# Moving the softmax division of the last stage from the weights to the weighed heads, with transposed reciprocals

## What is computed

```python
def attention(q, k, v, mask):
    scores = jnp.einsum('bhqd,bhkd->bhqk', q, k) / jnp.sqrt(jnp.float32(HD))
    scores = scores * mask - 10000.0 * (1.0 - mask)
    probs = jax.nn.softmax(scores, axis=-1)
    return jnp.einsum('bhqk,bhkd->bhqd', probs, v)
...
ctx = merge_heads(attention(split_heads(q), split_heads(k), split_heads(v), ltor_mask))
attn_out = ctx @ w_ao + b_ao
x = hidden_states + attn_out
...
ctx = merge_heads(attention(split_heads(q), split_heads(k), split_heads(v), cross_mask))
cross_out = ctx @ w_co + b_co
x = x + cross_out
```

## Time and profile before

| | |
|---|---|
| median of 3 runs | 1036.88 us (1036.30 to 1036.94) |
| profiled execution, its own time | 1035.47 us |
| its span in the trace | 1034.2 us |
| PE, PEld busy | 1000.6 us (97%), 900.8 us (87%) |
| DVE, ACT, POOL busy | 767.9 us (74%), 577.0 us (56%), 651.7 us (63%) |
| granted TensorE clock, mean | 1.00 |

### The profile page before, as it was taken

The page is one execution under the profiler, slowest core; times in us unless marked ns, Lnnn a source line. Parts: engine busy times, 40 slices in busy tenths (PEclk is TensorE's granted clock), DMA queues, the critical chain, the costliest instruction groups (busy, mean ns, idle before and its releaser), DMA issues.

```text
span 1034.2 us, 21141 instructions
## 1 busy us (share of the span) xinstructions
PE 1000.6 (97%) x8239; PEld 900.8 (87%) x8239; DVE 767.9 (74%) x1229; ACT 577.0 (56%) x1288; POOL 651.7 (63%) x595
## 2 busy tenths in 40 slices
PE   7899999999999999999998999999998999989998
PEld 7788888888899999999997999999998988777877
DVE  7997888998257677876767867777865387898761
ACT  5998888797534422223233332222226489999982
POOL 6885476755578574434367666755534388999960
PEclk9999999999999999999999999999999999999999
DMA  8200001000121220121120111110120000000000
GB/s 329 119 2 2 1 2 42 2 1 2 47 77 42 72 82 28 56 82 42 41 85 21 42 42 42 34 38 12 31 103 1 1 2 1 2 2 2 12 11 21
DMA packets 33931, 40.73 MB, mean 39 GB/s; under 512 B 2127, under 2 KB 31273, under 8 KB 32297
## 3 DMA queue, kind: packets, MB, share of 16 engines
q1 hardware_dynamic: 33833, 39.38, 11.4%
HBM read 38.32 MB, written 1.05 MB: 38 GB/s over the span
## 4 chain that ended last, share of the span: by engine, by line
PE 81%; POOL 9%; DVE 4%; ACT 4%; issue 1%; DMA 0%; SPq 0%; DVEq 0%; ACTq 0%; POOLq 0%
PE psum L914 11%; PE psum L793 9%; PE psum L809 9%; PE psum L946 8%; PE psum L994 8%; PE psum L981 6%; PE psum L928 5%; PE psum L960 5%; PE psum L835 5%; POOL C tile L1792 3%; PE psum L720 3%; PE psum L970 3%; PE psum L825 3%; PE psum L850 2%; POOL C tile L1798 2%; PE psum L864 1%
## 5 line engine op out<-in xcount | busy, mean ns | idle before, releaser
L1929 POOL TENSOR_TENSOR B tile<-B tile,B rec 128x1024 f32<-128x1024 f32 x32 | 61.0, 1909 | 161.6 <-DVE B rec L1351 161.6
L1798 POOL TENSOR_TENSOR A tile<-A tile,outer rec 128x1024 f32<-128x1024 f32 x48 | 91.0, 1905 | 57.9 <-DVE outer rec L1190 57.8
L1655 ACT COPY B PT<-psum 128x512 f32<-128x512 f32 x64 | 32.9, 601 | 139.0 <-PE psum L970 139.0
L1072 DVE TENSOR_SCALAR B qT<-psum,cols 128x1024 f32<-128x1024 f32 (+1 forms) x38 | 44.0, 1166 | 71.6 <-PE psum L914 70.2
L1570 ACT ACTIVATE A tile<-A tile,outer min 128x128 f32<-128x128 f32 (+1 forms) x256 | 92.2, 448 | 2.6 <-DVE outer min L1183 2.5
L1570 ACT ACTIVATE C tile<-C tile,outer min 128x128 f32<-128x128 f32 x256 | 77.9, 399 | 0.5 <-DVE outer min L1183 0.4
L946 PE MATMUL psum<-B v hi,cT hi 128*128 128x256 f32 x256 | 72.1, 282 | 0.3 <-ACT B kT L1485 0.3
L946 PE MATMUL psum<-B v hi,cT lo 128*128 128x256 f32 x256 | 71.8, 281 | 0.0
L946 PE MATMUL psum<-B v lo,cT hi 128*128 128x256 f32 x256 | 71.8, 281 | 0.0
L1798 POOL TENSOR_TENSOR C tile<-C tile,outer rec 128x1024 f32<-128x1024 f32 x32 | 60.5, 1895 | 6.0 <-DVE outer rec L1190 6.0
L1176 DVE TENSOR_TENSOR A tile<-m,psum 128x1024 f32<-128x1024 f32 x48 | 56.5, 1216 | 9.2 <-PE psum L825 8.0
(11 more groups left out here) (327 smaller groups left out, 3470.5 us busy)
## 6 DMA issues: line engine op xcount, KB each, us to landing
weights<-in_weights_c SPq DMA_DIRECT2D x5, 1024.0 KB, 6.3
raw<-in_wq SPq DMA_DIRECT2D x32, 128.0 KB, 2.7
raw<-in_wk SPq DMA_DIRECT2D x32, 128.0 KB, 3.0
raw<-in_wv SPq DMA_DIRECT2D x16, 256.0 KB, 2.8
raw<-in_wo SPq DMA_DIRECT2D x16, 256.0 KB, 2.7
weights<-in_weights_a SPq DMA_DIRECT2D x1, 3072.0 KB, 21.6
weights<-in_weights_a SPq DMA_DIRECT2D x1, 2048.0 KB, 12.4
wide<-in_bias_v SPq DMA_DIRECT2D x2, 1024.0 KB, 10.3
```

The costliest lines, as they stand in the source:

```text
L1798: pool.tensor_tensor(tile(u, ly.nk), tile(u, ly.nk), part.rec[:, u % 4, 0:ly.per].unsqueeze(2).to_broadcast([P, ly.per, ly.nk]), ALU.mult) ...
L1929: pool.tensor_tensor(tv, tv, m.brec[:, h, :].unsqueeze(2).to_broadcast([P, B, S]), ALU.mult).then_inc(s["normalised"].sem, s["normalised"] ...
```

## The change

In stage C the exponentials are transposed undivided: `turn` waits for ACT's exponentials alone. POOL no longer multiplies the tile; it spreads the 8 reciprocals of a half over rec_rows (queries by head features), in two copies of 128 x 64. PE transposes the two 128 x 128 blocks of rec_rows in `weigh`, behind the products, into the other half of bank 6, after a wait for POOL's copies of both halves. ACT copies that half of the bank to rec_rows (128 x 256) in place of the two copies with bias, and DVE multiplies the heads in PSUM by it into OT (128 x 256). The values' bias, which no longer goes into OT, is multiplied by the output weights once (`rows`: four matmuls on PE, one addition on DVE of 128 x 512) and added to the output's rows. `rows 4` is put ahead of `turn_in M2 mlp 0` on PE, and `output 3` is moved ahead of it too. DVE's list gets 16 `weigh` steps. Stage A is as before.

```diff
@@
-HEADS_ON = {"A": "DVE", "C": "ACT"}
+HEADS_ON = {"A": "DVE", "C": "DVE"}
@@
+            self.Cs.rec_rows = sc("C rec rows", [P, 2, C, P])
@@
     "PE": """
-    output 0, output 1, output 2, turn_in M2 mlp 0 7, output 3, turn_in M2 mlp 1 1, up M2 0 0 4, up M2 0 2 5, up M2 0 4 1, up M2 0 6 2,
+    output 0, output 1, output 2, output 3, rows 4, turn_in M2 mlp 0 7, turn_in M2 mlp 1 1, up M2 0 0 4, up M2 0 2 5, up M2 0 4 1, up M2 0 6 2,
@@
     "DVE": """
...
+    stats M2 mlp 2, stats M2 mlp 3, rows 4, xn M2 mlp 2, turn_in M2 mlp 2 1, down M2 0 0 2, down M2 0 1 1, stats L3s in 0, xn M2 mlp 3, xn L3s in 0,
...
+    scores 2, turn_in L3s in 2 7, minima 2, weigh 0, scores 3, weigh 1, project 0 4, even 2 0, q L3s 2 0, minima 3, even 2 1, scores 4, even 3 0,
...
+    minima 12, weigh 11, project 10 2, project 11 1, turn_in L3c mlp 1 0, stats L3c in 3, even 12 0, xn L3c in 3, down L3c 0 0 3, minima 13,
+    down L3c 0 1 7, even 12 1, even 13 0, q L3c 3 2, even 13 1, scores 14, minima 14, weigh 12, scores 15, project 12 4, even 14 0, minima 15,
+    even 14 1, weigh 13, project 13 7, even 15 0, stats L3c mlp 2, even 15 1, xn L3c mlp 2, turn_in L3c mlp 2 2, weigh 14, down L3c 1 0 0,
+    project 14 7, down L3c 1 1 1, weigh 15, project 15 7, stats L3c mlp 3, xn L3c mlp 3, turn_in L3c mlp 3 7, down L3c 2 0 1, down L3c 3 0 2,
@@ PE
         def turn(n, r):
-            pe.wait_ge(s["evened"].sem, s["evened"].at((st, u)))
+            ready = "exp_made" if st == "C" else "evened"
+            pe.wait_ge(s[ready].sem, s[ready].at((st, u)))
@@ weigh
+            if st == "C":
+                pe.wait_ge(s["evened"].sem, s["evened"].at((st, 2 * n + 1)))
+                for c in range(C):
+                    i = pe.transpose(bank(6)[:, (C + c) * P:(C + c + 1) * P], part.rec_rows[:, n % 2, c, :], m.ident[:, :])
@@
+        def rows(z):
+            once("w_late_loaded", 32)
+            claim(z, "rows_made", "rows")
+            for n, name in enumerate(("L3s", "L3c")):
+                for c in range(C):
+                    i = pe.matmul(bank(z)[:, n * D:(n + 1) * D], layers[name].bv[:, c:c + 1].to_broadcast([P, P]), layers[name].wo[:, c, :],
+                                  start=c == 0, stop=c == C - 1)
@@ DVE
+            if st == "C" and n >= 2:
+                dve.wait_ge(s["evened"].sem, s["evened"].at((st, u - 4)))
@@ heads
+            if st == "C":
+                dve.wait_ge(s["rec_copied"].sem, s["rec_copied"].at(("C", n)))
+                dve.tensor_tensor(part.OT[b][:, :, :], bank(6)[:, 0:C * P].rearrange("p (c q) -> p c q", c=C), part.rec_rows[:, n % 2, :, :], ALU.mult).then_inc(
+                    s["heads_drained"].sem, s["heads_drained"].mark((ly.name, k, b)))
+                return
@@ ACT
+            elif what == "weigh" and st == "C":
+                act.wait_ge(s["weighed"].sem, s["weighed"].at((st, a[0])))
+                act.copy(part.rec_rows[:, a[0] % 2, :, :], bank(6)[:, C * P:2 * C * P].rearrange("p (c q) -> p c q", c=C)).then_inc(
+                    s["rec_copied"].sem, s["rec_copied"].mark((st, a[0])))
@@ POOL, even
+            if st == "C":
+                if n >= 2:
+                    pool.wait_ge(s["heads_drained"].sem, s["heads_drained"].at((units[n - 2][0].name, *units[n - 2][1:3])))
+                for c in range(C):
+                    i = pool.tensor_copy(part.rec_rows[:, n % 2, c, r * 4 * HD:(r + 1) * 4 * HD].rearrange("p (j q d) -> p j q d", j=2, q=2),
+                                         part.rec[:, u % 4, :].rearrange("p (j c q) -> p j c q", j=2, c=C)[:, :, c, :].unsqueeze(3).to_broadcast([P, 2, 2, HD]))
+                i.then_inc(s["evened"].sem, s["evened"].mark((st, u)))
+                return
```

More of the change, by code:

```diff
@@ L176 @@
     "bq_drained", "bk_drained", "bv_drained", "bshifted", "own_made", "summed", "normalised", "ot_hi", "ot_lo", "o_projected",
-    "o_added", "x_biased",
+    "o_added", "x_biased", "rows_projected", "rows_made", "rec_copied",
     "product_made", "product_copied", "products_added", "form_made", "forms_hi", "forms_lo", "half_made", "half_ended", "halves_hi", "halves_lo",
@@ L612 @@
     output 0, stats M2 mlp 0, output 1, xn M2 mlp 0, stats M2 mlp 1, output 2, xn M2 mlp 1, turn_in M2 mlp 0 7, output 3, turn_in M2 mlp 1 1,
-    stats M2 mlp 2, stats M2 mlp 3, xn M2 mlp 2, turn_in M2 mlp 2 1, down M2 0 0 2, down M2 0 1 1, stats L3s in 0, xn M2 mlp 3, xn L3s in 0,
-    turn_in L3s in 0 2, q L3s 0 1, scores 0, scores 1, minima 0, down M2 1 0 5, minima 1, down M2 1 1 1, stats L3s in 1, turn_in M2 mlp 3 7, xn L3s in 1,
-    even 0 0, even 0 1, turn_in L3s in 1 5, down M2 2 0 4, even 1 0, down M2 2 1 7, stats L3s in 2, even 1 1, q L3s 1 7, xn L3s in 2, scores 2,
@@ L616 @@
[L616 to L623, removed]
@@ L624 @@
-    stats L3c mlp 2, even 15 1, xn L3c mlp 2, turn_in L3c mlp 2 2, down L3c 1 0 0, project 14 7, down L3c 1 1 1, project 15 7, stats L3c mlp 3,
-    xn L3c mlp 3, turn_in L3c mlp 3 7, down L3c 2 0 1, down L3c 3 0 2, down L3c 2 1 0, down L3c 3 1 7
+    stats M2 mlp 2, stats M2 mlp 3, rows 4, xn M2 mlp 2, turn_in M2 mlp 2 1, down M2 0 0 2, down M2 0 1 1, stats L3s in 0, xn M2 mlp 3, xn L3s in 0,
+    turn_in L3s in 0 2, q L3s 0 1, scores 0, scores 1, minima 0, down M2 1 0 5, minima 1, down M2 1 1 1, stats L3s in 1, turn_in M2 mlp 3 7,
@@ new lines @@
+    xn L3s in 1, even 0 0, even 0 1, turn_in L3s in 1 5, down M2 2 0 4, even 1 0, down M2 2 1 7, stats L3s in 2, even 1 1, q L3s 1 7, xn L3s in 2,
+    scores 2, turn_in L3s in 2 7, minima 2, weigh 0, scores 3, weigh 1, project 0 4, even 2 0, q L3s 2 0, minima 3, even 2 1, scores 4, even 3 0,
+    project 1 1, minima 4, even 3 1, stats L3c in 0, even 4 0, weigh 2, down M2 3 0 7, xn L3c in 0, scores 5, project 2 7, even 4 1, minima 5,
+    weigh 3, project 3 3, stats L3c in 1, q L3c 0 0, even 5 0, xn L3c in 1, down M2 3 1 7, scores 6, stats L3s in 3, even 5 1, minima 6, weigh 4,
@@ new lines @@
+    scores 7, even 6 0, xn L3s in 3, project 4 0, minima 7, even 6 1, q L3c 1 7, even 7 0, weigh 5, scores 8, project 5 7, stats L3c in 2, even 7 1,
+    turn_in L3s in 3 2, minima 8, weigh 6, scores 9, even 8 0, even 8 1, minima 9, q L3s 3 1, project 6 7, xn L3c in 2, even 9 0, weigh 7, scores 10,
+    even 9 1, project 7 7, stats L3c mlp 0, minima 10, weigh 8, scores 11, xn L3c mlp 0, even 10 0, q L3c 2 1, minima 11, even 10 1,
+    turn_in L3c mlp 0 5, weigh 9, project 8 7, even 11 0, project 9 7, scores 12, stats L3c mlp 1, even 11 1, xn L3c mlp 1, weigh 10, scores 13,
@@ L626 @@
+    down L3c 2 1 0, down L3c 3 1 7
 """,
@@ L852, in weigh @@
                                           start=(odd, src) == (0, 0), stop=odd == 1 and src == ly.n_src - 1)
+            if st == "C":
+                pe.wait_ge(s["evened"].sem, s["evened"].at((st, 2 * n + 1)))
+                for c in range(C):
+                    i = pe.transpose(bank(6)[:, (C + c) * P:(C + c + 1) * P], part.rec_rows[:, n % 2, c, :], m.ident[:, :])
             i.then_inc(s["weighed"].sem, s["weighed"].mark((st, n)))
+        def rows(z):
[5 more added lines that the diff above has]
+                                  start=c == 0, stop=c == C - 1)
+            i.then_inc(s["rows_projected"].sem, s["rows_projected"].mark("rows"))
         def project(n, z):
@@ L890, in do @@
                 project(*a)
+            elif what == "rows":
+                rows(*a)
             elif what == "keys_of":
@@ L1257, in do @@
                 output(2, NP_ - 1, a[0])
+            elif what == "rows":
+                at = ROWS.index("L3_b_ao")
+                dve.wait_ge(s["rows_projected"].sem, s["rows_projected"].at("rows"))
+                dve.tensor_tensor(m.rows[:, at:at + 2, :], m.rows[:, at:at + 2, :], bank(a[0]).rearrange("p (n d) -> p n d", n=2), ALU.add).then_inc(
+                    s["rows_made"].sem, s["rows_made"].mark("rows"))
         return do
@@ L1774, in residual @@
             row = UP[name][3] if of == "mlp" else layers[name].row
+            if st == "C" and of == "attn":
+                pool.wait_ge(s["rows_made"].sem, s["rows_made"].at("rows"))
             pool.tensor_tensor(part.xb[k][:, :, :], m.x(k), m.row(row).unsqueeze(1).to_broadcast([P, SB, D]), ALU.add).then_inc(
```

## The result

| | before | after |
|---|---|---|
| median, same chip | 1036.59 us (4 runs) | 1053.87 us (4 runs) |
| ratio, 95% interval | | 1.017 (1.0157 to 1.0183) |
| profiled execution, span | 1035.47, 1034.2 us | 1053.54, 1052.3 us |
| DVE, ACT, POOL busy | 767.9, 577.0, 651.7 us | 773.7, 575.3, 605.3 us |

The change costs 17.3 us. The sign was forecast, the size was not: 8.0 us were expected, and the result lies above the range. POOL is relieved of 46 us, more than the 33 expected, and the kernel is slower all the same.

The account below looks back on a forecast made before the run. From 864 to 946 the chain passes through POOL but ACT has least room; then PE, ACT's exponentials and PE again bind. Terms +1.3, +2.6, -2.5, +2.4, +4.2 sum to +8.0: 1044.9 us against the median, range 1036 to 1051.

Parts of the forecast that it names:

- Start: Start of stage C: `output 3` and `rows` delay the first transposes, DVE's addition costs nothing; +1.3 us.
- unit 1: `weigh 1` waits for bank 6, freed by DVE's `weigh 0` queued behind `minima 2`; +2.6 us.
- the end: Last units: `weigh 13` stands behind `even 14 1` on DVE, so `project 13` and ACT's copy come later; +4.2 us.
- Long stretch: 864.2 to 946.3: POOL relieved, ACT saves 0.21 us a unit, two thirds of ACT's limit taken; -2.5 us.
- Rival (c): DVE becomes the bound, keeping its waiting in the long stretch and adding 4.1 us: 1051.5 us; chance 15%.
- 946 to 983: PE has no room: added transposes, and `project 11` waits for DVE's `weigh 11` behind masks and minima; +2.4 us.
- (a): Faster: DVE reaches `weigh 0`, `11` and `13` before PE needs them, ACT alone sets the pace; 1030.1 us; chance 12%.
- (b): No change: the waits take back just what ACT gives; 1037 us; chance 8%.
- (d): POOL's copies cost 1.85 us a pair, so POOL stays full, no gain in the long stretch; 1047.4 us; chance 7%.
- (e): The clock falls to 1.2 GHz from 920 to 946.3, where PE does transposes; some +18 us, 1063; chance 1%.

Follow-up runs that it names:

- the bias row: Kernel before with the values' bias put in the output's rows and one ACT head copy, division on POOL: 1034.78 us; with the division also left out: 1033.27 us.
- all places early: Kernel after with the three_places edits, PE's old start order with `rows 0` behind it, and five more `weigh` steps earlier in DVE's list: 1038.99 us, 1.0032 over before.
- weigh13_early: Kernel after with DVE's `weigh 13` put ahead of the minima of unit 15 and the sum behind them: 1049.97 us, 1.0137 over before.
- weigh0_early: Kernel after with DVE's `weigh 0` put ahead of the minima of unit 2, directly behind the masks: 1050.78 us, 1.014 over before.
- heads_on_dve: Kernel before with the head drains with bias moved from ACT to DVE, at the change's places in DVE's list; division stays on POOL: 1049.78 us, 1.0142.
- rows_bank0: Kernel after with the product of the bias rows in bank 0 instead of bank 4: 1050.26 us, 1.0149 over before.
- three_places: Kernel after with the edits of rows_bank0, weigh0_early and weigh13_early together: 1042.87 us, 1.0068 over before.
- dve_heads_early: heads_on_dve with DVE's `weigh` 0, 3, 5, 9, 12, 13 and 14 at earlier places; division still on POOL: 1040.8 us, 1.0051 over before.

## Why the prediction was wrong

**Start: the step that failed.** "Two things stand in front of it ... `rows` is 1.7" is right, as a piece of the chain after shows:

```profile
789.72 1.73 PE psum L868 x8
```

What failed is "DVE's addition ... costs nothing: DVE is busy 7.47 of 25.60 us there". The busy share was no answer to the question who waits for the addition. `rows 4` and `up M2 0 0 4` name the same bank in one line of the diff; the claim makes PE wait for DVE, and DVE reaches that step 5 us after the product. It cost 3.6 to 3.9 us, shown by the run with bank 0. What should have been priced is the time until DVE's list comes to `rows`, not DVE's 0.7 us.

**The clock: a term that was missing.** Some 4.6 us are products at the lower level behind gaps that the change opens. The prediction had two of them in its own list (3 us before `weigh 1`, 4 before `project 13`) and argued about the clock only in the stretch from 920 to 946, where PE has many short gaps, which is where it did not fall. Whether the clock falls behind such a gap was not the same in each execution, so this term is a range, from nothing to 2.9 us a gap, and not a fixed price. With the clock's part taken off, unit 1 is 4.0 - 1.3 = 2.7 for 2.6 predicted, and the end 6.3 - 1.8 = 4.5 for 4.2: these two mechanisms and their sizes were right.

**Long stretch: the sign was wrong.** The term of -2.5 took two thirds of what ACT's idleness allows and gave DVE's 4.1 us of new work no price, since DVE had 8.9 us of idleness. POOL's relief was worth 1.8 us here with nothing else in its way (the bias row with and without division), less than its 3.7 us of waits suggest, and 1.35 with the reciprocals' path in its place. DVE's heads at these places took 3.35, of which 1.4 were late places. Together that is +2.0 from `weigh 2` to `weigh 11`, where the term said -2.5. The 8.9 us of DVE's idleness were waits in the middle of an ordered list, so they were no room for steps that somebody waits for. Rival (c), DVE as the bound, comes nearer: its +4.1 is about twice what was measured, its sign is right. In the stretch after the change DVE is busy 77.29 of 87.00 us, so it is not full either; it is late.

**946 to 983** was right: +1.9 for 2.4, by the wait for ACT's copy and the two minima. The transposes of the reciprocals cost 0.37 us a pair in the chain where 0.22 was taken.

**The rivals.** (a) wanted the waits of `weigh 1`, `project 11` and `project 13` under 6 us together, and then a gain. With all places early they are, and the kernel is still 3.3 us slower; (a) and (b) are out. (d) and (e) are out by the rows above.

In sum, against the profiled spans, which hold the clock's part of that one execution (+18.1 for +8.0): 4.6 for the clock, 2.3 for bank 4 without its clock part, 4.3 for the long stretch, 0.4 for what is left of unit 1 and the end, less 0.5 for 946 to 983 and less the 0.58 by which stage C began earlier. This is 10.5, of 10.1 that were missed. What stays open: whether another order of ACT's steps (its copy of reciprocals ahead of the transposed tiles) would shorten the chain at 957. It was not tried.

## What to carry to other kernels

Price a moved or added step by who waits for its buffer next, bank by bank, and by how far down the list the engine is that has to free it; the engine's idle share doesn't answer this. When work is taken from an engine that is in the chain only now and then, measure its floor by leaving the work out: here 60 us of POOL's time were worth 2 us. And when an edit opens a long gap on PE, look at the granted clock right behind it, in more than one execution.

## What the runs showed of the hardware

- The granted clock fell behind waits of PE, but not each time, and the length of the wait did not decide it alone. Each row is one profiled execution:

| PE waited, us | where | clock in the stretch behind it |
|---|---|---|
| 4.77, 4.77, 4.78 | before the first `up` (after, weigh13_early, weigh0_early) | 0.81, 0.81, 0.71 in 9 us |
| 3.03, 3.44 | before `weigh 1` (after, heads_on_dve) | 0.72, 0.72 in 6 us |
| 3.02, 3.02 | before `weigh 1` (rows_bank0, weigh13_early) | 1.00, 1.00 in 6 us |
| 3.41, 3.46, 3.38 | before `project 13` (after, heads_on_dve, rows_bank0) | 0.79, 0.79, 0.59 in 8 us |
| 3.39 | before `project 13` (weigh0_early) | 1.00 in 8 us |
| 2.32 | before the first `up` (three_places) | 0.81 in 9 us |
| 2.33 | before the first `up` (rows_bank0) | 1.00 in 9 us |
| 1.41 | before a `turn` (dve_heads_early) | 0.72 in 6 us |

- What decides between two executions with the same wait, no run here shows. The Trainium skill ("TensorE: Matmul & The Clock Gate", Part 1) names idleness as what brings the slower level back; the traces agree for the three waits of 4.8 us, and show that shorter ones can be followed by it or not. In the kernel after, products of 256 columns started 0.213 us apart (797.97, 798.18, 798.39), which is the level of 1.2 GHz, and from 800.66 on 0.12 us apart (800.66, 800.78, 800.90), the level of 2.4.
- The statement of the Trainium skill ("TensorE: Matmul & The Clock Gate", Part 4) that transposes do not count as PE activity like products was rival (e) and did not decide: with all 32 added transposes the all-places version runs at a mean clock of 1.00.
- Where the clock fell behind a wait of 3 us or more, it cost 1.3 to 2.9 us more in the products behind it: the 48 products that take 5.80 us took 7.25, 7.44 and 8.24 behind the same 4.8 us, and behind the 3.38 us in rows_bank0 the projection took 2.08 and the 16 products 5.26 against 1.03 and 3.45. So the wait itself is not the whole price.
- POOL's copy of 128 x 64 with a broadcast source took 0.244 us, less than the 0.265 of its 128 x 1 instruction: 64 columns cost no more than one; 256 columns took 0.925.
